# When the next batches' gate statistics are taken in a scan and expert kernel: split, moved behind the shared sums, with GpSimd's base additions held back

## The chip, the core and the metric

The kernel runs on one core of one Trainium2 chip. The metric is the device time of one execution in microseconds. Each kernel is run several times and the median counts; lower is better.

## What is computed

The input x is 4 batches of 512 tokens by 512 features. The first layer is a selective scan over the context, gated by SiLU of the normalized x; its result is added to x. The second layer normalizes again, runs two shared experts on all tokens and the two best of 16 routed experts on each token, and adds both:

```python
x = x + _L0_xattn_ref(ctx_1024, _layernorm(x, axis=-1), ...)   # scan output times silu(layernorm(x))
x = x + _L0_ffn_ref(_layernorm(x, axis=-1), ...)
# inside _L0_ffn_ref, with xn the normalized input:
aff = sigmoid(xn @ wa);  topk_p, topk_i = top_k(aff, 2)        # routing
routed = einsum('bsed,bse->bsd', experts(xn), combine)
shared = sum over 2 shared experts of w2(gelu(xn g + gb) * (xn w1 + b1)) + b2
return xn + shared + routed
```

## The kernel before, in words

The program has one instruction list for each engine, written out by hand, and semaphores between them: an instruction that waits holds up all that stands behind it on its engine. It has three stages. The first is projections and the scan (64 steps, to about 430 us). The second, the middle stage from about 430 to 640 us, goes through the four batches b = 0 to 3, each of four tiles of 128 tokens (16 tiles in all). The third runs 47 blocks of routed experts and adds their rows to the output.

The change lies in the middle stage. What each engine does there for batch b:

- **VectorE**, `first_norm(b)`: mean and variance of x for the gate (four BN_STATS of L930, four BN_AGGR of L933, then variance plus epsilon, L936), then a wait for GpSimd's reciprocal root (L454, `rstd_first(b)`), then the shift, minus mean times root (L938). ScalarE's `gates(b)` (L739, four SiLU activations with that scale and shift) waits for it.
- **TensorE**, `turn_gates(b)` (L1461): 16 transposes of the gates to PSUM; **VectorE**, `gate_tiles(b)` (L1017): four products of the scan's output with the transposed gates; `residual(b)` (L1025, L1027, L1029): adds x and takes the second norm's statistics; `variance(b)` (L1033); then GpSimd's `rstd_second(b)` (L496); then `normed(b)` (L1045), four tiles of the normalized tokens xn.
- **TensorE**, `turn_normed(b)` (L1489); ScalarE and VectorE split its result in two parts (`turn_normed` L749, `token_rests` L1053).
- The shared experts: TensorE's `up_shared(i)`, four of them for a batch (i = 0 to 15), 24 matmuls each; ScalarE's `gelu(i)` (L756) and `hidden_heads(i)` (L763); VectorE's `hidden_shared(i)` (L1066) and `hidden_rests(i)` (L1059). Then the down product, 12 matmuls (L1497, L1498, L1499) for a tile, into one of two PSUM banks by turns: `down_two_tiles(0, range(2))` for tiles 0 and 1, `down_shared(0, range(2, 4))` for tiles 2 and 3. VectorE's `add_shared` (L1075) adds each tile's sum out of its bank to `acc`; **TensorE starts a tile only when the tile two before it has been added**, since it needs that bank.
- **GpSimd**, `base(b)`: eight additions (L502 of xn, L504 of the shared bias, by turns) that make `acc` the base of the output. `add_shared` waits for those of its own batch.
- `logits(b)` on TensorE (12 matmuls with `wa_head`, `wa_rest`) needs all gates of batch b+1 applied; its 16 rows are copied by ScalarE (`copy_scores` L768), transposed by TensorE (L1516) and copied again (`copy_logits` L772).

The order on VectorE and GpSimd around the change is this (the rest is in the listing):

```python
            first_norm(2)
            first_norm(3)
            add_shared(0, every)
            gate_tiles(2)
...
            base(0)
            rstd_second(1)
            rstd_first(2)
            base(1)
            rstd_first(3)
            rstd_second(2)
            base(2)
```

Of the kernel before, what the change touches and what calls it, by code (L numbers as in the profile page):

```python
# [33 lines left out]
LT = L // P  # L34
# [16 lines left out]
def bass_xattn_scan_moe_kernel(nc, x, ctx_t, in_proj_t, conv_w, conv_b, x_proj_t, dt_proj_t, dt_b,  # L51
# [6 lines left out]
    with ExitStack() as ctx:  # L58
# [82 lines left out]
        def one_pass(ap):  # L141

            return ap.bitcast(F32R)
# [144 lines left out]
        def since(eng, semaphore, count):  # L288

            if not (isinstance(count, int) and count <= 0):  # L290
                eng.wait_ge(semaphore, count)
# [122 lines left out]
        def _(pool):  # L414
            s = S
# [34 lines left out]
            def rstd_first(b):  # L450

                pool.wait_ge(s["ln1_var"], b + 1)
                since(pool, s["gate_ready"], EC * b)
                pool.tensor_tensor(rstd[:], var_eps[:], minus_half[:], ALU.pow).then_inc(s["ln1_rstd"], 1)  # L454
# [39 lines left out]
            def rstd_second(b):  # L494
                pool.wait_ge(s["ln2_var"], b + 1)
                pool.tensor_tensor(rstd2[:], var_eps2[:], minus_half[:], ALU.pow).then_inc(s["ln2_rstd"], 1)  # L496

            def base(b):
                for i, lt in enumerate(TILES[b]):
                    t = b * LT + lt  # L500
                    pool.wait_ge(s["xn_ready"], b * LT + i + 1)
                    pool.tensor_tensor(acc[:, t], acc[:, t], xn[b % 2][:, lt], ALU.add).then_inc(s["base_xn"], 1)  # L502
                    pool.wait_ge(s["base_xn"], b * LT + i + 1)
                    pool.tensor_tensor(acc[:, t], acc[:, t], sb2_sb[:, 0], ALU.add).then_inc(s["base_ready"], 1)  # L504
# [10 lines left out]
            rstd_second(1)  # L515
            rstd_first(2)
            base(1)
            rstd_first(3)
            rstd_second(2)
            base(2)  # L520
            rstd_second(3)
            base(3)
# [54 lines left out]
        def _(act):  # L577
            s = S
# [154 lines left out]
            def gates(b):  # L733
                act.wait_ge(s["ln1_ready"], b + 1)
                if b == 0:
                    act.wait_ge(s["decay_ready"], EC * STEPS)
                since(act, s["gt_ready"], LT * b)
                for ec in range(EC):
                    act.activation(gates_of[b][:, ec], xb[b % 2][:, ec], ACT.Silu, bias=shift[:, ec:ec + 1],  # L739
                                   scale=rstd[:, ec:ec + 1]).then_inc(s["gate_ready"], 1)  # L740

            def turn_normed(b):
                for i, lt in enumerate(TILES[b]):
                    act.wait_ge(s["xnt_ready"], b * LT + i + 1)
                    if b >= 2:

                        act.wait_ge(s["sh_ready"], SH * FC * (b - 1))
                        act.wait_ge(s["scores_ready"], b - 1)
                    act.copy(one_pass(x_head[b % 2][:, :, lt * P:(lt + 1) * P]), ps[:, SIDE_BANK[lt]].rearrange(  # L749
                        "p (k n) -> p k n", n=P)).then_inc(s["xnt_copied"], 1)  # L750

            def gelu(i):
                q = i % (SH * FC)
                act.wait_ge(s["sh_ready"], i + 1)
                since(act, s["sy_ready"], i - 1)
                act.activation(sg[:, i % 2], ps[:, 2 * (i % 2)], ACT.Gelu,  # L756
                               bias=sbg_sb[:, q // FC, q % FC:q % FC + 1]).then_inc(s["sg_ready"], 1)

            def hidden_heads(i):
                q = i % (SH * FC)  # L760
                act.wait_ge(s["sy_ready"], i + 1)
                since(act, s["so_ready"], LT * (i // (SH * FC)))
                act.copy(one_pass(sy_head[:, q]), raw_hidden(i)).then_inc(s["syh_made"], 1)  # L763

            def copy_scores(b):
                act.wait_ge(s["scores_ready"], b + 1)
                since(act, s["logits_ready"], LT * (b - 1))
                act.copy(scores[b % 2], ps[0:E, SIDE_BANK[1]]).then_inc(s["scores_copied"], 1)  # L768
# [24 lines left out]
            gelu(4)  # L793
            gelu(5)
            hidden_heads(4)
            gates(3)
            copy_scores(1)
            copy_logits(1, 1)
            gelu(6)
            hidden_heads(5)  # L800
            turn_normed(2)
            gelu(7)
            hidden_heads(6)
            gelu(8)
# [79 lines left out]
        def _(dve):  # L884
            s = S
# [13 lines left out]
            def one_and_lost(b):  # L899
                e_b, one_b = e_abs[:, b % 2], one_e[:, b % 2]  # L900
                dve.wait_ge(s["exp_made"], b + 1)
                since(dve, s["delta_ready"], b - 1)
                dve.tensor_scalar(one_b, e_b, 1.0, None, ALU.add).then_inc(s["onep_made"], 1)
                dve.wait_ge(s["onep_made"], b + 1)
                dve.scalar_tensor_tensor(out=e_b, in0=one_b, scalar=-1.0, in1=e_b, op0=ALU.add,
                                         op1=ALU.subtract).then_inc(s["lost_made"], 1)

            def less_lost(b):
                dve.wait_ge(s["lost_made"], b + 1)
                dve.wait_ge(s["relu_made"], EC * (b + 1))  # L910
                dve.tensor_tensor(delta[:, b], delta[:, b], e_abs[:, b % 2], ALU.subtract).then_inc(s["relu_less"], 1)
# [11 lines left out]
                dve.wait_ge(s["dskip_made"], EC * (b + 1))  # L923
                dve.tensor_tensor(u[:, b], delta[:, b], u[:, b], ALU.mult).then_inc(s["du_made"], 1)

            def first_norm(b):

                dve.wait_ge(s["x_odd" if b % 2 else "x_even"], 16 * (b // 2 + 1))
                for ec in range(EC):
                    dve.bn_stats(stats[:, ec], xb[b % 2][:, ec]).then_inc(s["ln1_stat"], 1)  # L930
                dve.wait_ge(s["ln1_stat"], EC * (b + 1))
                for ec in range(EC):
                    dve.bn_aggr(meanvar[:, ec], stats[:, ec]).then_inc(s["ln1_aggr"], 1)  # L933
                dve.wait_ge(s["ln1_aggr"], EC * (b + 1))
                since(dve, s["gate_ready"], EC * b)
                dve.tensor_scalar(var_eps[:], meanvar[:, :, 1], EPS, None, ALU.add).then_inc(s["ln1_var"], 1)  # L936
                dve.wait_ge(s["ln1_rstd"], b + 1)
                dve.scalar_tensor_tensor(out=shift[:], in0=meanvar[:, :, 0], scalar=-1.0, in1=rstd[:],  # L938
                                         op0=ALU.mult, op1=ALU.mult).then_inc(s["ln1_ready"], 1)
# [6 lines left out]

            one_and_lost(0)
            less_lost(0)
            first_norm(0)
            one_and_lost(1)  # L950
            add_logarithm(0)
            delta_u(0)
# [82 lines left out]
            def normed(b):  # L1035
                dve.wait_ge(s["ln2_rstd"], b + 1)
                if b == 0:
                    dve.wait_ge(s["y_turned"], EC * STEPS)
                if b >= 2:

                    dve.wait_ge(s["xn_odd_stored" if b % 2 else "xn_even_stored"], 16 * LT * (b // 2))
                    dve.wait_ge(s["xnt_ready"], LT * (b - 1))
                    dve.wait_ge(s["base_xn"], LT * (b - 1))
                for lt in TILES[b]:
                    dve.tensor_scalar(xn[b % 2][:, lt], acc[:, b * LT + lt], meanvar2[:, lt, 0:1], rstd2[:, lt:lt + 1],  # L1045
                                      ALU.subtract, ALU.mult).then_inc(s["xn_ready"], 1)
# [14 lines left out]
            def hidden_shared(i):  # L1061
                q = i % (SH * FC)
                dve.wait_ge(s["sg_ready"], i + 1)
                if i not in AHEAD_OF_DOWN:
                    since(dve, s["so_ready"], LT * (i // (SH * FC)))
                dve.scalar_tensor_tensor(out=raw_hidden(i), in0=ps[:, 2 * (i % 2) + 1],  # L1066
                                         scalar=sb1_sb[:, q // FC, q % FC:q % FC + 1], in1=sg[:, i % 2],
                                         op0=ALU.add, op1=ALU.mult).then_inc(s["sy_ready"], 1)

            def add_shared(b, tiles):  # L1070
                for lt in tiles:
                    t = b * LT + lt
                    dve.wait_ge(s["so_ready"], t + 1)
                    dve.wait_ge(s["base_ready"], LT * (b + 1))
                    dve.tensor_tensor(acc[:, t], ps[:, 6 + lt % 2], acc[:, t], ALU.add).then_inc(s["so_added"], 1)  # L1075
# [126 lines left out]
            every, early, late = range(LT), range(LT // 2), range(LT // 2, LT)  # L1202
# [2 lines left out]
            variance(0)  # L1205
            normed(0)
            token_rests(0)
            first_norm(1)
            hidden_shared(0)
            gate_tiles(1)  # L1210
            residual(1, early)
# [8 lines left out]
            hidden_rests(2)  # L1220
            token_rests(1)
            hidden_rests(3)
            first_norm(2)
            first_norm(3)
            add_shared(0, every)
            gate_tiles(2)
            residual(2, early)
            hidden_shared(4)
# [2 lines left out]
            hidden_shared(5)  # L1231
            hidden_rests(4)
            normed(2)
            hidden_shared(6)
            hidden_rests(5)
            token_rests(2)
# [524 lines left out]
```

## Time and profile before

| what | value |
|---|---|
| median of 3 runs | 918.79 us (918.78 to 921.83) |
| profiled execution, its own time | 924.07 us |
| its span in the trace | 922.3 us |
| busy: TensorE / VectorE / ScalarE / GpSimd | 88% / 72% / 60% / 56% |

The profile is of one execution. Times in the trace count from the start of its span; 1.8 us of the execution's time lie outside it. PE is TensorE, PEld its weight loads, DVE VectorE, ACT ScalarE, POOL GpSimd, SP the queue that issues loads and stores. A matmul of 512 columns is shown with its modelled end, so that neighbours overlap: their pace is the distance of their starts.

### The profile page before, as it was taken

What the parts mean: (1) busy time and instruction counts of PE and PEld (TensorE: products, weight loads), DVE (VectorE), ACT (ScalarE), POOL (GpSimd) and SP (SyncE); (2) the same over time, 40 slices, a digit from 0 to 9 for tenths busy, and PEclk for the clock granted to TensorE, in tenths of its full rate; (3) what the DMA queues carried; (4) which work ended last, traced back from release to release, by engine and by line L of the source; (5) the groups of instructions that cost most, each with busy time, mean ns of one, the idle gap of its engine ahead of it and who ended that gap; (6) DMA issues with size and microseconds to landing.
All of it is one profiled execution on the core that took longest, in us unless ns stands there. A gap on an engine that the chain in (4) does not pass through costs nothing.

```text
span 922.3 us, 16039 instructions
## 1 busy us (share of the span) xinstructions
PE 815.4 (88%) x4380; PEld 594.0 (64%) x4381; DVE 663.1 (72%) x858; ACT 557.0 (60%) x927; POOL 520.0 (56%) x326
## 2 busy tenths in 40 slices
PE   6987489999999988996885999999999899989992
PEld 2323378888888878886764778886555455545550
DVE  4859889999999998999584585825555565545551
ACT  3588499999999999994331422113554455545541
POOL 2310079999999999997813542022254535356432
PEclk9976699999999999999897999999999999999997
DMA  5010031111141113201220112059367787777773
GB/s 169 0 51 1 1 125 56 55 56 54 59 139 56 58 47 104 59 12 56 83 92 0 46 47 92 6 177 411 81 172 221 181 212 173 203 177 211 181 166 50
DMA packets 32424, 95.44 MB, mean 103 GB/s; under 512 B 5088, under 2 KB 5216, under 8 KB 29040
## 3 DMA queue, kind: packets, MB, share of 16 engines
q1 hardware_dynamic: 20400, 65.37, 21.1%
q0 software_dynamic: 11968, 29.37, 14.7%
q8 instruction: 30, 0.49, 0.2%
q14 instruction: 26, 0.21, 0.1%
HBM read 122.11 MB, written 21.36 MB: 156 GB/s over the span
## 4 chain that ended last, share of the span: by engine, by line
PE 45%; DVE 17%; DMA 16%; POOL 9%; issue 8%; ACT 3%; POOLq 1%; DVEq 0%; SPq 0%; ACTq 0%
DVE r L979 12%; DMA out<-sg,ids 7%; DMA out<-sb_sb,ids 6%; PE ps L1497 6%; PE ps L1499 6%; PE ps L1498 6%; POOL r L464 5%; PE ps L1422 5%; PE ps L1446 5%; PE ps L1671 3%; PE ps L1353 3%; PE ps L1423 3%; PE ps L1652 3%; PE ps L1361 2%; DMA r<-xn_scratch,ids 2%
## 5 line engine op out<-in xcount | busy, mean ns | idle before, releaser
L464 POOL TENSOR_TENSOR r<-r,mem 128x1024 f32<-128x1024 f32 x126 | 295.2, 2384 | 55.5 <-DMA mem<-cm_rows 51.8
L979 DVE TENSOR_TENSOR_SCAN r<-r,ps 128x1024 f32<-128x1024 f32 x128 | 286.9, 2277 | 15.8 <-issue 10.2
L684 ACT ACTIVATE r<-mem,nega 128x511 f32<-128x511 f32 x256 | 167.1, 711 | 1.1 <-DVE r L979 1.1
L1422 PE MATMUL ps<-ident,mem 128*128 128x128 f32 x768 | 131.5, 281 | 30.3 <-DVE r L979 22.4
L1446 PE MATMUL ps<-ident,r 128*128 128x128 f32 x1024 | 132.6, 273 | 1.2 <-POOL r L464 1.0
L696 ACT ACTIVATE mem<-mem,bc 128x512 f32<-128x512 f32 x192 | 124.6, 712 | 10.0 <-PE ps L1423 9.4
L1422 PEld LDWEIGHTS ps<-ident,mem 128*128 128x128 f32 x768 | 88.3, 143 | 55.6 <-issue 53.3
L1446 PEld LDWEIGHTS ps<-ident,r 128*128 128x128 f32 x1024 | 115.8, 141 | 2.0 <-POOL r L464 1.5
L1423 PE MATMUL ps<-mem 128*128 128x128 f32 x512 | 100.7, 279 | 0.0
L1671 PE MATMUL ps<-mem 128*128 x188 | 92.3, 616 | 2.0 <-ACT mem L846 1.4
L1497 PE MATMUL ps<-split 128*128 128x512 f32 x192 | 78.8, 411 | 16.3 <-DVE acc L1075 12.2
L1652 PE MATMUL ps<-r,picked 128*128 x188 | 88.3, 592 | 0.0
L1423 PEld LDWEIGHTS ps<-mem 128*128 128x128 f32 x512 | 79.0, 195 | 0.0
L569 POOL DMA_INDIRECT out<-sg,ids x24 | 38.9, 1620 | 68.9 <-DMA out<-sg,ids 28.0
L1499 PE MATMUL ps<-split 128*128 128x512 f32 x192 | 76.9, 400 | 0.0
L1498 PE MATMUL ps<-split 128*128 128x512 f32 x192 | 76.7, 399 | 0.0
L569 POOL DMA_INDIRECT out<-sb_sb,ids x23 | 37.5, 1629 | 66.2 <-DMA out<-sb_sb,ids 30.7
L1278 DVE TENSOR_TENSOR acc_again<-r,acc_again 128x1024 fp32r<-128x1024 f32 x47 | 57.6, 1226 | 20.5 <-issue 20.2
L537 POOL DMA_INDIRECT r<-xn_scratch,ids x47 | 53.3, 1134 | 31.9 <-PE ps L1638 19.0
L837 ACT CAST acc_again<-r 128x1024 fp32r x47 | 49.0, 1046 | 33.2 <-issue 21.1
L756 ACT ACTIVATE sg<-ps,sbg_sb 128x512 f32<-128x512 f32 x16 | 10.9, 689 | 92.8 <-PE ps L1499 92.8
L846 ACT COPY mem<-ps 128x256 f32<-128x256 f32 x47 | 17.5, 372 | 68.9 <-PE ps L1660 68.7
(195 smaller groups left out, 1323.0 us busy)
## 6 DMA issues: line engine op xcount, KB each, us to landing
r<-in_r_up SPq DMA_DIRECT2D x47, 1024.0 KB
mem<-in_r_down SPq DMA_DIRECT2D x47, 512.0 KB
mem<-cm_rows SPq DMA_DIRECT2D x64, 256.0 KB, 3.3
mem<-in_r_b SPq DMA_DIRECT2D x4, 2048.0 KB, 14.0
r<-in_x SPq DMA_DIRECT2D x4, 1024.0 KB, 4.8
xn_scratch<-r SPq DMA_DIRECT2D x16, 256.0 KB, 2.8
out<-acc POOLq DMA_DIRECT2D x16, 256.0 KB, 2.9
mem<-in_ctx_t SPq DMA_DIRECT2D x4, 512.0 KB, 8.3
```

The costliest lines, as they stand in the source:

```text
L464: pool.tensor_tensor(state[:, k % 2, ec:ec + 2], state[:, k % 2, ec:ec + 2], c, ALU.mult).then_inc(s["weighed"], 1)
L684: act.activation(decay[:, k % 2, ec, 1:L], delta[:, b, ec, 1:L], ACT.Exp, scale=nega[:, ec, n:n + 1]).then_inc(s["decay_ready"], 1)
L696: act.activation(dbu_t[:, k % 2, lt], du_t[:, t], ACT.Copy, scale=bc[:, t, DR + k % DS:DR + k % DS + 1]).then_inc(s["dbut_made_a"], 1)
L979: dve.tensor_tensor_scan(state[:, half, ec:ec + 2].rearrange("p e l -> p (e l)"), decay[:, half, ec:ec + 2].rearrange("p e l -> p (e l)"), ...
L1422: pe.transpose(ps[:, ec, lt * P:(lt + 1) * P], dbu_t[:, k % 2, lt, ec * P:(ec + 1) * P], ident[:])
L1423: pe.matmul(ps[:, ec, (LT - 1) * P:LT * P], du_t[:, k // DS * LT + LT - 1, ec * P:(ec + 1) * P], b_diag[k % 2], start=True, stop=True).the ...
L1446: mm = pe.matmul(ps[:, Y_BANK + lt, ec * P:(ec + 1) * P], state[:, k % 2, ec, lt * P:(lt + 1) * P], ident[:], is_transpose=True, start=Fal ...
L1497: pe.matmul(to, one_pass(l_head), one_pass(r_head), start=(first and i == 0), stop=False)
L1498: pe.matmul(to, one_pass(l_head), one_pass(r_rest), start=False, stop=False)
L1499: mm = pe.matmul(to, one_pass(l_rest), one_pass(r_head), start=False, stop=(last and i == n - 1))
L1652: mm = pe.matmul(ps[:, r % 2], xgt[:, r % 2, (kc - KSPLIT) * P:(kc - KSPLIT + 1) * P], up_weights(slot_j, kc, kc + 1), start=False, stop=( ...
L1671: mm = pe.matmul(ps[:, 6 + r % 2], hyt[:, r % 2, fc * P:(fc + 1) * P], down_weights(slot_j, fc), start=(fc == 0), stop=(fc == FC - 1))
```

## The change

VectorE's `first_norm(b)` becomes two functions: `first_stats(b)`, which ends with the variance, and `first_shift(b)`, which waits for GpSimd's root and makes the shift. For batches 0 and 1 they are called one right after the other, as before. For batch 2 the sums of tiles 0 and 1 are added between them and those of tiles 2 and 3 behind. For batch 3 both are moved behind `normed(2)`. On ScalarE `gates(3)` moves from behind `hidden_heads(4)` to behind `turn_normed(2)`. On GpSimd `rstd_second(2)` and `rstd_first(3)` change places, and each `base(b)` waits once, for all four tiles of xn of its batch, where it waited tile by tile.

```diff
             def base(b):
+                pool.wait_ge(s["xn_ready"], LT * (b + 1))
                 for i, lt in enumerate(TILES[b]):
                     t = b * LT + lt
-                    pool.wait_ge(s["xn_ready"], b * LT + i + 1)
                     pool.tensor_tensor(acc[:, t], acc[:, t], xn[b % 2][:, lt], ALU.add).then_inc(s["base_xn"], 1)
...
             base(1)
+            rstd_second(2)
             rstd_first(3)
-            rstd_second(2)
             base(2)
...
             hidden_heads(4)
-            gates(3)
             copy_scores(1)
             copy_logits(1, 1)
             gelu(6)
             hidden_heads(5)
             turn_normed(2)
+            gates(3)
             gelu(7)
...
-            def first_norm(b):
+            def first_stats(b):
...
                 dve.tensor_scalar(var_eps[:], meanvar[:, :, 1], EPS, None, ALU.add).then_inc(s["ln1_var"], 1)
+
+            def first_shift(b):
+
                 dve.wait_ge(s["ln1_rstd"], b + 1)
...
             hidden_rests(3)
-            first_norm(2)
-            first_norm(3)
-            add_shared(0, every)
+            first_stats(2)
+            add_shared(0, early)
+            first_shift(2)
+            add_shared(0, late)
             gate_tiles(2)
...
             normed(2)
+            first_stats(3)
+            first_shift(3)
             hidden_shared(6)
```

VectorE where the sums of batch 0 are added, before: `x4` is four instructions of a kind; BN_STATS of `r` is the statistics of x, `acc<-ps,acc` of L1075 the sums, of L1017 the gate products.

```order
L936 TENSOR_SCALAR var_eps<-meanvar 128x4
L938 SCALAR_TENSOR_TENSOR shift<-meanvar,rstd 128x4
L930 BN_STATS stats<-r 128x6 x4
L933 BN_AGGR meanvar<-stats 128x2 x4
L936 TENSOR_SCALAR var_eps<-meanvar 128x4
L938 SCALAR_TENSOR_TENSOR shift<-meanvar,rstd 128x4
L1075 TENSOR_TENSOR acc<-ps,acc 128x512 x4
L1017 TENSOR_TENSOR acc<-ps,acc 128x512 x4
```

The same place in the changed kernel, whose lines from here on have numbers four higher (three for the shift):

```order
L936 TENSOR_SCALAR var_eps<-meanvar 128x4
L1079 TENSOR_TENSOR acc<-ps,acc 128x512 x2
L941 SCALAR_TENSOR_TENSOR shift<-meanvar,rstd 128x4
L1079 TENSOR_TENSOR acc<-ps,acc 128x512 x2
L1021 TENSOR_TENSOR acc<-ps,acc 128x512 x4
```

Two sums now stand ahead of batch 2's shift, and nothing of batch 3 stands ahead of any sum.

VectorE after `variance(2)` in the changed kernel, where batch 3's part has gone; L1049 is `normed(2)`, L1070 `hidden_shared`, L1063 `hidden_rests`:

```order
L1070 SCALAR_TENSOR_TENSOR mem<-ps,sb_sb,sg 128x512
L1063 TENSOR_TENSOR split<-mem,split 128x512
L1049 TENSOR_SCALAR r<-acc,meanvar,rstd 128x512 x4
L930 BN_STATS stats<-r 128x6 x4
L933 BN_AGGR meanvar<-stats 128x2 x4
L936 TENSOR_SCALAR var_eps<-meanvar 128x4
L941 SCALAR_TENSOR_TENSOR shift<-meanvar,rstd 128x4
L1070 SCALAR_TENSOR_TENSOR mem<-ps,sb_sb,sg 128x512
```

Before, the last row followed right on `normed(2)`.

ScalarE, the difference from `hidden_heads(4)` on; ACT_TABLE_LOAD changes between the tables of SiLU and GELU, the four ACTIVATE of L739 are `gates(3)`:

```order
 L763 CAST split<-mem 128x512
+L768 COPY picked<-ps 16x512
+L772 COPY aff<-ps 128x64
+L756 ACTIVATE sg<-ps,sbg_sb 128x512
+L763 CAST split<-mem 128x512
+L749 CAST split<-ps 128x4x128 x4
 L739 ACT_TABLE_LOAD
 L739 ACTIVATE r<-r,shift,rstd 128x512 x4
-L768 COPY picked<-ps 16x512
-L772 COPY aff<-ps 128x64
 L756 ACT_TABLE_LOAD
-L756 ACTIVATE sg<-ps,sbg_sb 128x512
```

The gates of batch 3 and both table loads now stand between `turn_normed(2)` (L749) and `gelu(7)`; their number is the same.

GpSimd, the difference behind `base(1)`:

```order
 L502 TENSOR_TENSOR acc<-acc,r 128x512
 L504 TENSOR_TENSOR acc<-acc,sb_sb 128x512
-L454 TENSOR_TENSOR rstd<-var_eps,minus_half 128x4
-L496 TENSOR_TENSOR rstd<-var_eps,minus_half 128x4
+L496 TENSOR_TENSOR rstd<-var_eps,minus_half 128x4
+L454 TENSOR_TENSOR rstd<-var_eps,minus_half 128x4
 L502 TENSOR_TENSOR acc<-acc,r 128x512
```

The root for the second norm of batch 2 now comes ahead of the root for the gate of batch 3, and both still ahead of `base(2)`.

## Rows read from the trace of the kernel before

**Rows 1.** Whom TensorE waited for, 460 to 645 us: total, times, longest.

```profile
PE ps L1497 <- DVE acc L1075: 12.2, 1, 12.2
...
PE ps L1516 <- ACT picked L768: 0.5, 1, 0.5
```

**Rows 2.** Stretches: length, busy PE, PEld, DVE, ACT, POOL, clock, DMA share, GB/s.

```profile
481.80:494.00 12.20, 0.01 (x2) 0.01 (x1) 5.65 (x13) 4.21 (x5) 11.02 (x10) 0.62 0.00 0
494.00:498.40 4.40, 4.40 (x10) 3.46 (x11) 0.54 (x1) 0.00 (x0) 0.00 (x0) 0.51 0.00 0
498.40:560.00 61.60, 60.28 (x301) 46.26 (x300) 38.95 (x64) 18.97 (x31) 27.12 (x24) 1.00 0.15 56
560.00:656.00 96.00, 95.50 (x452) 75.31 (x451) 55.10 (x148) 23.36 (x45) 14.26 (x19) 0.98 0.41 159
656.00:922.30 266.30, 241.28 (x845) 138.51 (x843) 139.10 (x214) 127.73 (x255) 120.92 (x85) 0.97 0.70 173
```

**Rows 3.** Timeline of VectorE, 480 to 505 us: start, length, what, [idle before].

```profile
480.64 0.17 DVE L936 TENSOR_SCALAR var_eps<-meanvar 128x4 f32<-128x4 f32 x1
481.94 1.21 DVE L938 SCALAR_TENSOR_TENSOR shift<-meanvar,rstd 128x4 f32<-128x4 f32 x1 [1.12 <-POOL rstd L454]
...
486.22 0.85 DVE L936 TENSOR_SCALAR var_eps<-meanvar 128x4 f32<-128x4 f32 x1 [0.27 <-ACT r L739]
493.17 0.16 DVE L938 SCALAR_TENSOR_TENSOR shift<-meanvar,rstd 128x4 f32<-128x4 f32 x1 [6.11 <-POOL rstd L454]
493.25 1.29 DVE L1075 TENSOR_TENSOR acc<-ps,acc 128x512 f32<-128x512 f32 x2
```

**Rows 4.** Timeline of GpSimd: end of `base(0)`, start of `base(1)`, batch 3's root.

```profile
457.12 1.28 POOL L504 TENSOR_TENSOR acc<-acc,sb_sb 128x512 f32<-128x512 f32 x1
...
481.87 1.26 POOL L502 TENSOR_TENSOR acc<-acc,r 128x512 f32<-128x512 f32 x1
...
492.12 1.02 POOL L454 TENSOR_TENSOR rstd<-var_eps,minus_half 128x4 f32<-128x4 f32 x1
```

**Rows 5.** Timeline of TensorE at its waits.

```profile
476.12 0.47 PE L1497 MATMUL ps<-split 128*128 128x512 f32 x1 [1.66 <-issue]
...
480.74 0.39 PE L1499 MATMUL ps<-split 128*128 128x512 f32 x1
...
481.42 0.39 PE L1499 MATMUL ps<-split 128*128 128x512 f32 x1
494.00 0.79 PE L1497 MATMUL ps<-split 128*128 128x512 f32 x1 [12.19 <-DVE acc L1075]
...
530.88 1.91 PE L1461 MATMUL ps<-ident,r 128*128 128x128 f32 x16
```

**Rows 6.** Timeline of ScalarE, 515 to 532 us.

```profile
515.68 1.28 ACT L739 ACT_TABLE_LOAD   x1
516.97 2.94 ACT L739 ACTIVATE r<-r,shift,rstd 128x512 f32<-128x512 f32 x4
...
524.97 2.05 ACT L749 CAST split<-ps 128x512 fp32r<-128x512 f32 x4
531.09 0.69 ACT L756 ACTIVATE sg<-ps,sbg_sb 128x512 f32<-128x512 f32 x1 [4.06 <-PE ps L1499]
```

**Rows 7.** Timeline of VectorE: gate products, normalizations, and a `hidden_shared`.

```profile
457.50 2.47 DVE L1017 TENSOR_TENSOR acc<-ps,acc 128x512 f32<-128x512 f32 x4
...
469.67 1.91 DVE L1045 TENSOR_SCALAR r<-acc,meanvar,rstd 128x512 f32<-128x512 f32 x4 [0.48 <-POOL rstd L496]
...
516.45 3.87 DVE L1045 TENSOR_SCALAR r<-acc,meanvar,rstd 128x512 f32<-128x512 f32 x4
524.60 0.75 DVE L1066 SCALAR_TENSOR_TENSOR mem<-ps,sb_sb,sg 128x512 f32<-128x512 f32 x1 [4.28 <-ACT sg L756]
...
533.07 2.48 DVE L1017 TENSOR_TENSOR acc<-ps,acc 128x512 f32<-128x512 f32 x4
...
543.00 3.87 DVE L1045 TENSOR_SCALAR r<-acc,meanvar,rstd 128x512 f32<-128x512 f32 x4
```

More of the change, by code:

```diff
@@ L948, in _ @@
             less_lost(0)
-            first_norm(0)
+            first_stats(0)
+            first_shift(0)
             one_and_lost(1)
@@ L1207, in _ @@
             token_rests(0)
-            first_norm(1)
+            first_stats(1)
+            first_shift(1)
             hidden_shared(0)
```

## The prediction, made before the changed kernel was run

> **What bounds the kernel now.** I read TensorE's waits first. In the middle stage it has one large wait: 12.2 us for VectorE's sum of L1075, and nothing else near it [rows 1]. The table of stretches shows the same from outside: between 481.8 and 494.0 us TensorE does nothing while VectorE is busy for 5.65 us and GpSimd for 11.02 [rows 2]. In the 4.4 us behind it the granted clock is 0.51, TensorE's lower level of 1.2 GHz; from 498.4 to 560 it is 1.00, the upper level of 2.4 GHz, and TensorE is busy 60.28 of 61.60 us, then 95.50 of 96.00 to 656 us [rows 2]. So behind this one hole TensorE sets the pace until the experts run, and a microsecond taken out of the hole should move everything behind it, as long as the others keep up.
>
> VectorE's timeline tells what fills the hole. The reader should follow the order: batch 2's variance ends at 480.81, its shift comes at 481.94; batch 3's variance comes at 486.22; then VectorE stands still for 6.11 us until 493.17, waiting for GpSimd's root L454; only then come the sums, at 493.25 [rows 3]. GpSimd's timeline tells why the root is late: `base(1)` starts at 481.87 and the root of batch 3 is queued behind its eight additions, at 492.12 [rows 4]. TensorE had ended tiles 0 and 1 at 481.42 + 0.39 = 481.81, and started tile 2 at 494.00, right behind tile 0's sum [rows 5].
>
> **The hole, step by step.** Now the sums of tiles 0 and 1 stand right behind batch 2's variance, so VectorE is free for them from 480.81 [rows 3]. Tile 0's last matmul starts at 480.74 and ends at 481.13 [rows 5]. A sum takes about 0.69 us with its start-up (two take 1.29) [rows 3], so tile 0 is added at about 481.85 and tile 1 at 482.5. TensorE, done at 481.81, goes on at about 481.9. Gain: 494.0 - 481.9 = 12.1 us.
>
> **The clock.** Behind the hole ten matmuls take 4.4 us at the lower clock [rows 2]; at the pace before the hole, (481.42 - 480.74) / 3 = 0.227 us, they take 2.3 [rows 5]. That is 2.1 us more to gain if the clock stays up. A short pause does not take it down here: the one of 1.66 us before 476.12 is followed by matmuls of 0.39 us at 0.227 us distance [rows 5]. With 0.1 us instead of 12.2 I count the 2.1 us as gained.
>
> **Batch 2's gates.** The root of batch 2 is unchanged (the shift still waits for it, and base(1) starts at 481.87 as before [rows 4]). The shift took 1.21 us at 481.94, beside an addition of GpSimd that ran from 481.87 to 483.13, against 0.16 for the same shift at 493.17 with a root beside it [rows 3, 4]. Standing behind tile 1's sum it would end at about 483.2, as it did before: 0. ScalarE's gates then end near 486.1 (2.94 us, [rows 6]), and TensorE wants them after tiles 2 and 3, at 481.9 + 24 x 0.227 = 487.3. Hidden with 1.2 us to spare. Tile 3 is added at about 488.2, in time for `turn_gates(2)`'s last tile. The gate products follow, 2.5 us [rows 7]; the first residual addition behind them, near 490.8, can meet the last addition of `base(1)`, which ends at 492.1 [rows 4], and lose up to 1.3 us. Behind it stands `hidden_shared(4)`, which has to wait for the 24 matmuls of `up_shared(4)` in any case, to about 494.8, and whose reader is two up products away: 0.
>
> **GpSimd behind it.** `base(1)` still ends at 492.1. The root of batch 2's second norm is asked for ahead of `normed(2)` at 516.45 [rows 7], after the change some 14 us earlier, at 500 to 502. GpSimd has been idle for 7 us by then: 0.
>
> **Batch 3's part in its new place.** From here on times are those of before, since all is moved by the same amount. `normed(2)` takes 3.87 us with GpSimd's additions beside it, `normed(1)` 1.91 without [rows 7]. As `base(2)` now waits for all four tiles, it should take 1.9, to 518.4. Statistics and variance cost about 3.1 us (from 483.15, the end of one shift, to 486.22 [rows 3]), to 521.4; the root comes 1.3 us later (480.64 to 481.94 [rows 3]) and the shift may be held by the first addition of `base(2)`, so to 522.9 or 523.9. VectorE was idle for 4.28 us until 524.60 there [rows 7]: it fits, with 0.7 us left. What is queued behind the new wait is `hidden_shared(6)`, whose reader, TensorE's up product two further on, is 5 us away.
>
> **Batch 3's gates.** ScalarE ends `turn_normed(2)` at 524.97 + 2.05 = 527.02 [rows 6]. A table load, 1.28 us, and four gates, 2.94 [rows 6], end at 531.24. TensorE begins `turn_gates(3)` at 530.88 [rows 5], with weights loaded just ahead: it waits 0.4 to 0.6 us. Against that, `copy_scores(1)` no longer stands behind `gates(3)`, so the wait of 0.5 us of L1516 goes [rows 1], and it moves ScalarE earlier too. The two cancel: 0, give or take 0.3. The second load pushes `gelu(7)` from 531.09 [rows 6] to 532.5, 1.4 us late, and with it VectorE's gate products from 533.07 to 534.5, ending at 537.0 instead of 535.55 [rows 7]. TensorE needs them for `logits(2)`, which it reaches after 16 transposes and 24 matmuls, 530.88 + 1.9 + 5.4 = 538.2 (estimate from [rows 5]): 1.2 us to spare. `normed(3)` starts up to 1.5 us after 543.00 but takes 1.9 instead of 3.87 us [rows 7], so it ends at 546.4, before the 546.87 of now. `base(3)` starts 3 us later relative to the rest; the stores and loads behind it wait for later things.
>
> The row has the SiLU load at 515.68 with 1.28 us and the first gate at 516.97, right on its end [rows 6]. The Trainium skill, "ScalarE: Activation LUTs", section "What ACT_TABLE_LOAD costs", puts a switch at about 2.66 us, since a drain of 1.38 us follows the load. By that page, as an estimate, `gates(3)` would end 1.4 us later and the gain be 12.8 instead of 14.2; the trace here does not agree.
>
> **Sum.** 12.1 + 2.1 + 0 = 14.2 us. The profiled execution's own time is 924.07, so 909.9 for it. That execution was 5.3 us above the median; the hole is a matter of order, not of that surplus, so I take the same 14.2 from the median: 918.79 - 14.2 = **904.6 us**, 1.5% faster. About 0.5% (4.6 us) is what a measurement of this kernel can tell from no change.
>
> **Rivals.**
> - **Held gates.** The load and gates in their new place cost more than their rows say, for instance 1.4 us more before the first gate; TensorE then waits about 2 us at `turn_gates(3)`. For: it is the tightest new meeting, with no slack at all. Against: the row at 516.97. Gain 12.8, 906.0 us. Chance 0.05.
> - **The clock falls elsewhere.** A lower clock for about 4 us comes back at another place, for instance at the 0.5 us waits or in the routing. For: 560 to 656 has a mean of 0.98, so there is one such place already [rows 2]. Gain 12.1, 906.7 us. Chance 0.07.
> - **The sums still come late.** VectorE's sums or batch 2's shift run slower beside `base(1)`, so that TensorE loses 3 to 5 us of the 14. Against: the gate products have the operands of the sums, and beside `base(0)`'s additions at 457.50 [rows 4] they took 2.47 us, without any at 533.07 the same 2.48 [rows 7]. 908 to 910 us. Chance 0.05.
> - **The expert stage takes it back.** From 656 us on TensorE is busy 241.28 of 266.30 us and the DMA share is 0.70 [rows 2]; if that stage kept its end whatever its start, up to all 14 us would go. Against: all its loads are released by events of the middle stage. 911 to 919 us. Chance 0.05, half of it within 0.5%.
> - **No hole closed.** Another wait of the same kind, for instance of TensorE for the gates of batch 2, takes its place at once: 918 us. It needs these gates 12 us later than ScalarE can give them; nothing in rows 3 and 6 says so. Chance 0.02.
> - **Slower.** The mechanism is batch 3's shift behind `normed(2)`. ScalarE reaches its gates at 528.3, the shift is there by 523.9. Each microsecond beyond 528.3 holds TensorE at `turn_gates(3)`; only a shift later than about 542.5 eats the 14.2 us, and 20 us later than reckoned gives 920 us and more. The root would have to stand behind `base(2)`, and it stands ahead. Chance 0.02.
> - **More than forecast**, 16 us and over, by fewer small waits: 0.02, about 902 us.
>
> The forecast has the rest, 0.72; its own range is 902 to 908, since the three runs shown lie up to 3 us apart.
>
> **The numbers.** The range 901 to 908.5 takes in the forecast, the held gates, the other clock and the larger gain, 0.86 less what the runs' own spread puts outside. Faster by over 0.5%, below 914.2: 0.72 + 0.05 + 0.07 + 0.05 + 0.02 and half of 0.05 = 0.935. Within 0.5%: 0.045. Slower: 0.02.
>
> **What the new profile would show.** TensorE's wait for L1079 (the old L1075) at about 481.8 below 0.5 us, and matmuls at 0.227 us distance with a granted clock of 1.00 through 482 to 498. VectorE's first two sums at about 481.2, its shift right behind. The 16 transposes of `turn_gates(2)` starting near 487.5. `normed(2)` and `normed(3)` at 1.9 us. `gates(3)` ending about when TensorE asks for it. The end of the middle stage 14 us earlier, and a last stage of unchanged length. I would be wrong if TensorE showed a new wait of over 1 us at L1461 or at the logits, if VectorE's sums took twice their time beside GpSimd, or if the last stage grew.

## The result, and the profile after

The changed kernel takes 904.24 us (median of 4 runs, 898.68 to 907.32) against 918.78 (median of 4, 915.33 to 921.83) beside it. The ratio is 0.9846, with a 95% interval of 0.9816 to 0.9876: 1.5% faster, 14.5 us by the medians, where 14.2 were forecast. Its profiled execution took 904.82 us, its span is 903.0.

TensorE's waits in the changed kernel, 440 to 645 us (total, times, longest); the first is the one at the start of the middle stage, which was there before and which I had not looked at:

```profile
PE ps L1497 <- DVE r L1049: 7.5, 1, 7.5
...
PE ps L1469 <- ACT r L739: 0.3, 1, 0.3
```

The wait of 12.2 us for the sum, and that of 0.5 for ScalarE's copy [rows 1], are gone; a new one of 0.3 us for the gates of batch 3 (L1469) has come. The stretches of [rows 2], in the new trace (busy PE, PEld, DVE, ACT, POOL, then clock, DMA share, GB/s):

```profile
481.80:494.00 12.20, 12.10 (x61) 9.91 (x61) 7.88 (x14) 4.22 (x5) 11.52 (x9) 1.00 0.00 0
484.00:546.00 62.00, 60.88 (x303) 46.57 (x303) 39.89 (x75) 22.34 (x36) 35.86 (x31) 1.00 0.11 40
546.00:642.00 96.00, 95.58 (x457) 74.95 (x455) 55.78 (x149) 24.89 (x46) 15.37 (x23) 1.00 0.44 170
```

Where TensorE was busy for 0.01 us of 12.2, it is busy for 12.10, at a granted clock of 1.00. VectorE at the same place, to be held against [rows 3] (this trace runs 1.1 us later up to here):

```profile
481.73 0.17 DVE L936 TENSOR_SCALAR var_eps<-meanvar 128x4 f32<-128x4 f32 x1
482.29 1.37 DVE L1079 TENSOR_TENSOR acc<-ps,acc 128x512 f32<-128x512 f32 x2 [0.39 <-PE ps L1507]
483.58 0.69 DVE L941 SCALAR_TENSOR_TENSOR shift<-meanvar,rstd 128x4 f32<-128x4 f32 x1
486.09 0.69 DVE L1079 TENSOR_TENSOR acc<-ps,acc 128x512 f32<-128x512 f32 x1 [1.82 <-PE ps L1507]
488.82 0.69 DVE L1079 TENSOR_TENSOR acc<-ps,acc 128x512 f32<-128x512 f32 x1 [2.04 <-PE ps L1507]
```

VectorE now waits for TensorE (0.39, 1.82, 2.04 us) and not the other way round. TensorE in the same stretch and at its two later meetings, against [rows 5]:

```profile
477.21 0.47 PE L1505 MATMUL ps<-split 128*128 128x512 f32 x1 [1.66 <-issue]
...
482.54 0.39 PE L1507 MATMUL ps<-split 128*128 128x512 f32 x1
483.04 0.50 PE L1505 MATMUL ps<-split 128*128 128x512 f32 x1
...
488.62 1.91 PE L1469 MATMUL ps<-ident,r 128*128 128x128 f32 x16
...
517.79 1.97 PE L1469 MATMUL ps<-ident,r 128*128 128x128 f32 x16 [0.29 <-ACT r L739]
...
536.63 0.50 PE L1505 MATMUL ps<-split 128*128 128x512 f32 x1 [0.83 <-DVE split L1057]
```

Tiles 0 and 1 end at 482.54 + 0.39 = 482.93, tile 2 starts at 483.04: 0.1 us.

**Two marks.** To compare all traces I cut each in three. H is the time up to the first matmul of the down product of batch 0, the one behind the wait of 1.66 us (476.12 before, 477.21 after). M runs from the end of tiles 0 and 1, 5.7 us later, to the first matmul behind the wait of 0.83 us for batch 3's token rests (549.69 before, 536.63 after). L is the rest of the span. From before to after, H grows by 1.1 us, M falls from 67.9 to 53.7, by 14.2, and L falls from 372.6 to 366.4, by 6.2: together the 19.3 us between the two spans. The medians differ by 14.5, so one of these numbers had to be scatter. The table has the traces of all runs.

| kernel | H | M | L | time, median (runs) |
|---|---|---|---|---|
| before | 476.1 | 67.9 | 372.6 | 918.78 (4) |
| changed | 477.2 | 53.7 | 366.4 | 904.24 (4) |
| e0, changed again | 478.6 | 53.7 | 363.2 | 900.91 (4) |
| e1, before, root first | 476.2 | 61.7 | 366.9 | 911.97 (10) |
| e2, changed, gates(3) in the old place | 477.5 | 63.2 | 365.2 | 912.41 (10) |
| e3, changed, batch 2 not split | 476.3 | 57.2 | 364.4 | 904.57 (4) |
| e4, changed, additions tile by tile | 478.2 | 53.7 | 364.7 | 903.18 (4) |
| e5, before, hole filled | 478.4 | 66.1 | 364.4 | 915.74 (10) |
| e6, changed, warm start | 475.7 | 53.7 | 364.6 | 901.54 (6) |
| e7, changed again | 476.0 | 53.7 | 364.6 | 905.97 (6) |
| e8, e6 again | 476.0 | 53.7 | 362.1 | 903.47 (6) |
| e9, e3 with the second wait filled | 477.3 | 55.6 | 363.8 | 904.20 (1) |
| e10, e3 with the first wait filled | 477.8 | 57.2 | 363.9 | 906.40 (1) |

M repeats to 0.1 us for one kernel (53.7 in three traces of the changed one). In the same three traces H moves by 2.6 us and L by 3.2. The reader should judge a change of this stage by M: the three medians of the changed kernel (904.24, 900.91 and 905.97) lie 5 us apart.

### The profile page after: what moved, and what is told of

Read it like the earlier page. It is cut to its first block, busy times and chain, and to the rows that moved or that the text cites. A ratio compares the mean times of both kernels' runs of the same rounds, so it can differ in the third digit from the quotient of the medians.

```text
span 903.0 us, 16039 instructions
## 1 busy us (share of the span) xinstructions
PE 809.5 (90%) x4380; PEld 589.3 (65%) x4381; DVE 659.1 (73%) x858; ACT 556.4 (62%) x927; POOL 521.0 (58%) x326
## 4 chain that ended last, share of the span: by engine, by line
PE 43%; DMA 17%; DVE 15%; issue 9%; POOL 9%; ACT 5%; POOLq 1%; DVEq 0%; SPq 0%; ACTq 0%
DVE r L983 11%; DMA out<-sg,ids 8%; DMA out<-sb_sb,ids 8%; PE ps L1505 6%; PE ps L1506 6%; PE ps L1507 6%; POOL r L464 5%; PE ps L1430 5%; PE ps L1454 5%; PE ps L1361 3%; PE ps L1431 3%; PE ps L1369 2%; PE ps L1679 2%; PE ps L1660 2%; ACT mem L696 2%
## 5 line engine op out<-in xcount | busy, mean ns | idle before, releaser
L464 POOL TENSOR_TENSOR r<-r,mem 128x1024 f32<-128x1024 f32 x126 | 295.2, 2380 | 57.2 <-DMA mem<-cm_rows 53.9
L1505 PE MATMUL ps<-split 128*128 128x512 f32 x192 | 77.4, 403 | 4.2 <-DVE split L1057 2.3
L1506 PE MATMUL ps<-split 128*128 128x512 f32 x192 | 75.6, 394 | 0.0
L1507 PE MATMUL ps<-split 128*128 128x512 f32 x192 | 75.4, 393 | 0.0
```

The lines of the kernel that those rows point to most:

```text
L464: pool.tensor_tensor(state[:, k % 2, ec:ec + 2], state[:, k % 2, ec:ec + 2], c, ALU.mult).then_inc(s["weighed"], 1)
L1505: pe.matmul(to, one_pass(l_head), one_pass(r_head), start=(first and i == 0), stop=False)
L1506: pe.matmul(to, one_pass(l_head), one_pass(r_rest), start=False, stop=False)
L1507: mm = pe.matmul(to, one_pass(l_rest), one_pass(r_head), start=False, stop=(last and i == n - 1))
```

## The experiments

The theory: VectorE's sums stood behind batch 3's shift, this behind a root queued on GpSimd behind eight additions; taking that away gives 12.1 us, and 2.1 more by the clock. The rivals: the gain comes from fewer collisions of VectorE and GpSimd, from the move on ScalarE, or from the expert stage.

**e0, the changed kernel again.**

> The changed kernel once more, as the yardstick. Two marks are read in each trace. M: from the modelled end of the last matmul of tiles 0 and 1 of batch 0 (481.81 us before, 482.93 after) to the first matmul behind the wait for batch 3's token rests (549.69 before, 536.63 after): 67.9 us before, 53.7 after. L: from that matmul to the span's end, 372.6 us before, 366.4 after. My theory: the change is worth the 14.2 us of M, and the 6.2 us of L are scatter from run to run of the expert stage, so L here lies anywhere from 365 to 374. Rival: the change shortens L too; then L is 366 to 367 here and in every kernel that keeps the new order.

M is 53.7 again, L is 363.2, below the 366 to 367 of the rival. Two kernels with the old order, e1 and e5, have an L of 366.9 and 364.4. So nothing shows that the change touches L. The times say the same: over all runs the mean is 918.1 for the kernel before (51 runs) and 903.3 for the changed one (14), 14.9 us apart, give or take 2.

The 372.6 of the first profile was a long execution (924.07 us, 5.3 over its median). A part of its surplus can be read from the clock. Between 550 and 870 us the clock falls to its lower level for some 3 us three times in that trace, twice in e1, once in those of the changed kernel and e4, and not at all in the other nine, e5 with the old order among them. The first fall in the kernel before (stretch as in [rows 2]):

```profile
574.00:576.00 2.00, 2.00 (x6) 1.52 (x6) 1.83 (x7) 0.00 (x0) 0.00 (x0) 0.50 0.00 0
```

TensorE had no wait around it: the trace shows none from 560 to 600 us. The ten matmuls from 573.04 us on take 3.97 us, where they take 2.3 at the usual distance, so one such fall costs some 1.6 us. Why it comes in some executions and not in others stays open, as does the rest of the surplus.

**e1, GpSimd's additions of batch 1 behind batch 3's root, in the kernel before.**

```diff
-            base(1)
             rstd_first(3)
+            base(1)
             rstd_second(2)
```

> The kernel before, with one line moved on GpSimd: base(1) stands behind batch 3's root instead of ahead of it. VectorE and ScalarE keep the old order. Theory (the root queued behind eight additions makes most of the hole): batch 2's shift no longer meets an addition (0.2 instead of 1.2 us), batch 3's variance comes at about 485.2, its root ends at 486.4, the first sum starts at 486.6, TensorE goes on at 487.3. Hole 5.5 us instead of 12.2, M about 61.2 with the lower clock behind the hole, 59.1 without; time 912 to 914. Rival (the hole is VectorE's own work, or the gain came from fewer collisions of VectorE with GpSimd): hole over 10 us, M over 66.

The hole is 6.5 us instead of 12.2, M 61.7, the time 911.97 us (ratio 0.9943, 0.9914 to 0.9971). VectorE and TensorE in this kernel:

```profile
485.25 0.17 DVE L936 TENSOR_SCALAR var_eps<-meanvar 128x4 f32<-128x4 f32 x1 [0.27 <-ACT r L739]
486.54 1.21 DVE L938 SCALAR_TENSOR_TENSOR shift<-meanvar,rstd 128x4 f32<-128x4 f32 x1 [1.12 <-POOL rstd L454]
487.67 1.27 DVE L1075 TENSOR_TENSOR acc<-ps,acc 128x512 f32<-128x512 f32 x2
```

```profile
488.40 0.80 PE L1497 MATMUL ps<-split 128*128 128x512 f32 x1 [6.52 <-DVE acc L1075]
```

One line on GpSimd takes half the hole away: the queue is the cause of that half. My 5.5 us were 1.0 short because I let batch 3's shift run freely; it met the first addition of `base(1)`, now right behind its root, and took 1.21 us. M fell by 6.2 us, 0.5 more than the hole, as the slow stretch behind it ends after 3.3 us (near 491.7) and not after 4.4. What is left of the hole is VectorE's own order: batch 3's statistics and shift still stand ahead of the sums, and e3 below shows what goes with them.

**e2, the changed kernel with gates(3) in its old place on ScalarE.**

```diff
             hidden_heads(4)
+            gates(3)
             copy_scores(1)
...
             turn_normed(2)
-            gates(3)
             gelu(7)
```

> The changed kernel with gates(3) back in its old place on ScalarE, behind hidden_heads(4). Theory: ScalarE stands at gates(3) until batch 3's shift (about 510.8), copies the scores at about 513.7, and TensorE, which wants them at 506.9, waits 7.4 us there and runs 4 us at the lower clock: M 53.7 + 7.4 + 2.1 = 63.2, time 912 to 915. Rival (the move on ScalarE is of no account): M within 0.5 of 53.7.

M is 63.2, as worked out, and the time 912.41 us. TensorE's wait and the slow matmul behind it:

```profile
514.43 0.61 PE L1524 MATMUL ps<-ident,picked 16*128 16x16 f32 x4 [7.23 <-ACT picked L768]
514.97 0.80 PE L1505 MATMUL ps<-split 128*128 128x512 f32 x1
515.56 0.63 PE L1506 MATMUL ps<-split 128*128 128x512 f32 x1
```

So without the move on ScalarE the change would give back 9.5 of its 14.2 us: what waits for a step that is moved has to move with it. What that move would bring by itself no run shows. The swap of the two roots on GpSimd has no run of its own either, and could not have one: with batch 3's variance behind `normed(2)`, a `rstd_first(3)` ahead of `rstd_second(2)` would wait for that variance, `normed(2)` stands ahead of it, and `normed(2)` waits for `rstd_second(2)`: the three would wait for each other.

**e3, the changed kernel without batch 2's split.**

```diff
             first_stats(2)
-            add_shared(0, early)
             first_shift(2)
+            add_shared(0, early)
             add_shared(0, late)
```

> The changed kernel with batch 2's shift ahead of all sums again (its statistics not in two parts; batch 3's stay behind normed(2)). Theory: the shift waits for its root to 483.0 and for GpSimd's first addition to 484.2, the first sum ends at 484.95, TensorE waits 2.0 us instead of 0.1 and keeps its clock: M 55.7, time 2 us over the changed kernel, too little to tell by medians of three. So 12.1 of the 14.2 us are batch 3's doing. Rival (splitting batch 2 is the main part): M over 60.

TensorE waits for 1.97 us, as expected, yet M is 57.2 and not 55.7. TensorE, then two stretches of this kernel (columns as in [rows 2]):

```profile
481.65 0.39 PE L1507 MATMUL ps<-split 128*128 128x512 f32 x1
484.01 0.50 PE L1505 MATMUL ps<-split 128*128 128x512 f32 x1 [1.97 <-DVE acc L1079]
484.35 0.40 PE L1506 MATMUL ps<-split 128*128 128x512 f32 x1
484.59 0.40 PE L1507 MATMUL ps<-split 128*128 128x512 f32 x1
484.82 0.52 PE L1505 MATMUL ps<-split 128*128 128x512 f32 x1
485.13 0.63 PE L1506 MATMUL ps<-split 128*128 128x512 f32 x1
```

```profile
484.00:486.00 2.00, 1.99 (x7) 1.56 (x8) 0.55 (x1) 2.00 (x4) 1.94 (x2) 0.74 0.00 0
486.00:488.50 2.50, 2.50 (x8) 2.00 (x7) 0.00 (x0) 1.60 (x2) 2.48 (x2) 0.53 0.00 0
```

After the pause three matmuls run at full pace; then the distance becomes 0.43 us until 488.1. The clock fell one microsecond after TensorE had resumed. So the split is worth 3.5 us (2.0 of waiting and 1.5 of clock), and 10.7 of the 14.2 come from taking batch 3's part away from the sums, with all that has to move with it. The median, 904.57, could not have told this.

**e9 and e10, which pause took the clock down.** The pause of 1.97 us comes 7.7 us behind another, of 1.66 us. e9 fills the later one, e10 the earlier, with matmuls that nobody reads:

```diff
             down_two_tiles(0, range(2))
+            for _ in range(8):
+                pe.matmul(ps[:, 0], one_pass(sup_head[:, 0, 0, 0:P]), one_pass(x_head[0][:, 0]), start=True, stop=True)
             down_shared(0, range(2, LT))
```

```diff
+            pe.wait_ge(s["sy_ready"], 3)
+            for _ in range(6):
+                pe.matmul(ps[:, 0], one_pass(sup_head[:, 0, 0, 0:P]), one_pass(x_head[0][:, 0]), start=True, stop=True)
             down_two_tiles(0, range(2))
```

> The kernel without batch 2's split (sums behind the shift), with 8 unread matmuls in TensorE's 2.0 us wait for the first sum. Theory (that wait, coming 7.7 us behind another of 1.7 us, takes the clock down): all matmuls behind it at 0.227 us distance, M 55.7 instead of 57.2. Rival (the drop has another cause): slow matmuls remain behind it, M 57.2.

> The same kernel without the split, the 2.0 us wait left as it is, and 6 unread matmuls in the 1.7 us wait ahead of the down product. If the 2.0 us pause alone takes the clock down, the slow matmuls stay and M is 57.2. If it takes both pauses, the clock stays up and M is 55.7.

e9 has M 55.6 and no slow matmul. e10 has M 57.2, and the slow ones stay. e9, then e10:

```profile
482.84 1.97 PE L1610 MATMUL ps<-split 128*128 128x512 f32 x8
485.01 0.50 PE L1505 MATMUL ps<-split 128*128 128x512 f32 x1 [0.19 <-DVE acc L1079]
485.35 0.39 PE L1506 MATMUL ps<-split 128*128 128x512 f32 x1
```

```profile
485.45 0.50 PE L1505 MATMUL ps<-split 128*128 128x512 f32 x1 [1.97 <-DVE acc L1079]
...
486.48 0.52 PE L1506 MATMUL ps<-split 128*128 128x512 f32 x1
486.79 0.63 PE L1507 MATMUL ps<-split 128*128 128x512 f32 x1
```

Filled, the pause of 1.97 us is not followed by a fall; filling the one of 1.66 us changes nothing. So the fall hangs on the later pause, as far as one trace of each kernel can tell. It is not a matter of the length alone: e6 and e8, below, have a pause of 1.98 us with no fall behind it. What else decides stays open.

**e4, the changed kernel with GpSimd's additions tile by tile.**

```diff
             def base(b):
-                pool.wait_ge(s["xn_ready"], LT * (b + 1))
                 for i, lt in enumerate(TILES[b]):
                     t = b * LT + lt
+                    pool.wait_ge(s["xn_ready"], b * LT + i + 1)
```

> The changed kernel with base(b) waiting tile by tile again, as before. Theory (the wait for all four tiles only moves additions out of the way of VectorE, and that time is hidden): normed(2) and normed(3) take 3.9 us each again instead of 1.9, batch 3's shift slips by 2 us into VectorE's idle time, M 53.7 to 54.4. Rival (fewer collisions are a good part of the gain): M 57 or more.

M is 53.7, as in the changed kernel. The one wait for four tiles, the part of the change that its title names last, is worth nothing measurable here. But my expectation missed half of what happens. VectorE's two normalizations in e4, and GpSimd between them:

```profile
504.55 1.91 DVE L1049 TENSOR_SCALAR r<-acc,meanvar,rstd 128x512 f32<-128x512 f32 x4
...
509.53 1.01 POOL L454 TENSOR_TENSOR rstd<-var_eps,minus_half 128x4 f32<-128x4 f32 x1 [6.57 <-DVE var_eps L936]
...
532.40 3.86 DVE L1049 TENSOR_SCALAR r<-acc,meanvar,rstd 128x512 f32<-128x512 f32 x4 [0.91 <-POOL rstd L496]
```

Only `normed(3)` takes 3.86 us again (1.92 in the changed kernel). `normed(2)` stays at 1.91: `base(2)` stands behind batch 3's root, and that root now waits for a variance behind `normed(2)`. It is the reordering that keeps `base(2)` away from `normed(2)`; the single wait only matters for `normed(3)`, whose 2 us are hidden.

**e5, the kernel before with its hole filled.** All waits stay; between tiles 1 and 2 TensorE runs 50 matmuls that nobody reads.

```diff
             down_two_tiles(0, range(2))
+            for _ in range(50):
+                pe.matmul(ps[:, 0], one_pass(sup_head[:, 0, 0, 0:P]), one_pass(x_head[0][:, 0]), start=True, stop=True)
             down_shared(0, range(2, LT))
```

> The kernel before, with 50 matmuls of 512 columns, whose result nobody reads, put into TensorE's hole behind tiles 0 and 1 (11.4 of 12.2 us). All waits stay. Theory (behind the hole 2.1 us are lost to the lower clock): granted clock 1.00 from 482 to 500, the next sum's matmuls at 0.227 us distance, M 67.9 - 2.1 = 65.8. Rival (the slow matmuls behind the hole have another cause, such as VectorE's or GpSimd's traffic): they stay at 0.43 us and M at 67.9.

Stretches of this kernel, the hole and what follows:

```profile
484.10:496.40 12.30, 11.26 (x50) 9.01 (x48) 5.71 (x13) 4.22 (x5) 11.18 (x10) 1.00 0.00 0
496.40:501.00 4.60, 4.55 (x20) 3.76 (x21) 1.29 (x2) 0.00 (x0) 0.00 (x0) 1.00 0.00 0
```

The clock stays at 1.00, against 0.51 behind the empty hole [rows 2], and M falls by 1.8 us, to 66.1. The matmuls are useless and the kernel is faster for them: 915.74 us against 917.21 (ratio 0.9970, 0.9951 to 0.9989). Of the 14.2 us some 2 are the clock's.

**e6 and e8, a warm start on top of the changed kernel.** The waits of the changed kernel point to the 7.5 us ahead of batch 0's transposes. The hole itself is the chain of the first normalization; what can be had is the slow clock behind it.

```diff
             pe.wait_ge(s["loaded_shared"], 16 * 4)
+            pe.wait_ge(s["wh_made"], len(SPLIT_AT))
+            pe.wait_ge(s["gated"], LT)
+            for _ in range(25):
+                pe.matmul(ps[:, 0], one_pass(sup_head_all[:, 0:P]), one_pass(sup_head_all[:, 0:L]), start=True, stop=True)
             turn_normed(0)
...
-            for c in range(2, 6):
+            for c in range(2, 4):
                 weight_rests(c)
             rstd_first(1)
+            for c in range(4, 6):
+                weight_rests(c)
```

> The changed kernel, and on top of it 25 matmuls of 512 columns, whose result nobody reads, in TensorE's 7.5 us wait for the first normalized tile (432.3 to 439.8), and GpSimd's root for batch 1's gate taken behind two of the four subtractions of weights instead of behind all four. Theory: the transposes of batch 0 (3.65 us at the lower clock) take 1.9, the wait for batch 0's token rests ends 1.7 us sooner, the first eight matmuls save 1.6 us: the middle stage starts 3.3 us sooner, M and L unchanged, time 3 us under the changed kernel. Rival: batch 1's gates or GpSimd's subtractions hold TensorE a little later, and less than 1 us is left.

> The changed kernel, side by side with the next run. M 53.7 and a time of 901 to 905. L is expected between 363 and 367 as in all traces but that of the kernel before, 372.6.

> The changed kernel with the 25 unread matmuls ahead of batch 0's transposes and GpSimd's root taken earlier, once more, side by side with the changed kernel. The trace of its first run has the middle stage 2.7 us shorter. Theory: its median lies 2 to 3.5 us under that of the changed kernel beside it. Rival (the saving is given back in the expert stage, or is only scatter): within 1 us of it.

e7 (changed), then e8:

```profile
438.79 3.65 PE L1497 MATMUL ps<-ident,r 128*128 128x128 f32 x16 [7.51 <-DVE r L1049]
443.93 0.77 PE L1505 MATMUL ps<-split 128*128 128x512 f32 x1 [1.49 <-DVE split L1057]
```

```profile
435.32 5.91 PE L1604 MATMUL ps<-split 128*128 128x512 f32 x25 [1.39 <-DVE acc L1023]
441.51 1.94 PE L1499 MATMUL ps<-ident,r 128*128 128x128 f32 x16 [0.28 <-DVE r L1051]
445.43 0.47 PE L1507 MATMUL ps<-split 128*128 128x512 f32 x1 [1.98 <-DVE split L1059]
```

The 16 transposes take 1.94 us instead of 3.65. From the first transpose of batch 0's gates to the first matmul of the down product it is 46.3 us in e6 (429.37 to 475.66) and e8 (429.73 to 476.04), and 48.9 in e0 (429.67 to 478.58): 2.6 us saved where I had 3.3, mostly since the wait for the token rests grew from 1.49 to 1.98. M and L do not answer. Side by side the medians are 903.47 and 905.97, 2.5 us apart; but the six runs of each lie from 899.34 to 909.45 and from 900.86 to 907.32, and over all runs the mean is 902.4 for the warm start (12 runs) and 903.3 for the changed kernel (14), 0.8 us apart, give or take 2.5. The traces show 2.6 us; the times agree with that and with nothing at all, so the 2.5 us between the two medians are no proof.

TensorE pauses for 1.98 us ahead of 445.43, and behind this pause the clock stays up (e8; e6 shows the same):

```profile
445.40:450.40 5.00, 4.97 (x22) 4.13 (x23) 3.81 (x10) 0.00 (x0) 4.17 (x3) 1.00 0.02 8
```

## Why the prediction was right

**The hole: right to 0.1 us.** I had TensorE wait 0.1 us behind tiles 0 and 1, and it waits 0.1. M fell by 14.2, the sum that I had. That the median, 904.24, came out 0.4 us from the forecast is luck: medians of this one kernel lie 5 us apart.

**The clock: right in the sum, thin in its reason.** The clock stayed up, and e5 shows about 2 us for it (1.8 against my 2.1). But I leaned on one pause of 1.66 us as proof that short pauses are harmless. In e3 and e10 the clock falls behind one of 1.97 us, in e6 and e8 not behind one of 1.98, and in the kernel before, near 574 us, it falls with no pause at all. So the length of a pause alone does not tell, and my reason was none. The gain held because the wait fell to 0.1 us; in e3, with VectorE 1.9 us later, 3.5 us went, not 2.

**Batch 2's gates: right.** The shift ended at 484.27, the 483.2 that I gave plus the 1.1 us by which this trace is later; it was held by an addition, 0.69 us instead of 0.16. TensorE began `turn_gates(2)` at 488.62 without a wait. ScalarE had ended the gates at 487.24, 1.4 us ahead, close to the 1.2 that I worked out; the 12 us of slack that I gave them under "No hole closed" contradict that and were wrong.

**Batch 3's part in its new place: right in the times, wrong in one reason.** `normed(2)` takes 1.91 us instead of 3.87 [rows 7], but not for the single wait in `base(2)` that I gave as the reason: e4, without it, has 1.91 too. The root ahead of `base(2)` holds it back. Further, the statistics end at 508.4, and the shift, held by the first addition of `base(2)` as I allowed, ends at 510.74. VectorE, from `normed(2)` on:

```profile
503.48 1.91 DVE L1049 TENSOR_SCALAR r<-acc,meanvar,rstd 128x512 f32<-128x512 f32 x4
505.30 2.46 DVE L930 BATCH_NORM_STATS2 stats<-r 128x6 f32<-128x512 f32 x4
...
508.21 0.17 DVE L936 TENSOR_SCALAR var_eps<-meanvar 128x4 f32<-128x4 f32 x1
509.50 1.24 DVE L941 SCALAR_TENSOR_TENSOR shift<-meanvar,rstd 128x4 f32<-128x4 f32 x1 [1.12 <-POOL rstd L454]
511.06 0.75 DVE L1070 SCALAR_TENSOR_TENSOR mem<-ps,sb_sb,sg 128x512 f32<-128x512 f32 x1 [0.32 <-ACT sg L756]
```

The margin was 0.32 us; I had 0.7.

**Batch 3's gates: right.** TensorE waits 0.29 us at L1469 and no longer at the copy of the scores (0.49 us before): the two cancel. ScalarE around it:

```profile
511.43 2.05 ACT L749 CAST split<-ps 128x512 fp32r<-128x512 f32 x4
513.50 1.28 ACT L739 ACT_TABLE_LOAD   x1
514.80 2.94 ACT L739 ACTIVATE r<-r,shift,rstd 128x512 f32<-128x512 f32 x4
517.75 1.28 ACT L756 ACT_TABLE_LOAD   x1
519.05 0.69 ACT L756 ACTIVATE sg<-ps,sbg_sb 128x512 f32<-128x512 f32 x1
```

Both loads are followed by an activation 0.02 us after their end. Each load begins right on the end of the instruction ahead of it, too (511.43 + 2.05 and 514.80 + 2.94). By the figures that I weighed from the Trainium skill, "ScalarE: Activation LUTs", section "What ACT_TABLE_LOAD costs", each load would be joined by a drain of 1.38 us, and TensorE would have waited for it; the trace does not agree.

**What I had not counted.** The title's last part, the single wait for four tiles, adds nothing (e4); I had taken its 2 us on VectorE as what made batch 3's part fit. The 2 us came from the reordering itself, so the fit with `normed(2)` at 3.87 us was never put to the test, and the margin of 0.32 us says nothing of more room. And I set the surplus of the profiled execution aside rightly: it was L, and 6 of the 19 us between the two profiles would have misled anyone who took the spans as the result.

## What to carry to other kernels

When an engine stands still for 12 us, follow the wait through two queues: the short step that is waited for may be queued behind long ones that nobody needs yet, and on the waiting engine the work that is due may stand behind a step that is not. Move the step that is not due, and with it whatever waits for it on other engines (e2: 9.5 us given back otherwise). Cut the trace at marks that all kernels share: here one stage repeats to 0.1 us, while whole runs scatter by several.

## What the runs showed of the hardware that I had not expected

- Behind a pause of TensorE of 1.97 us the clock fell from the upper level to the lower one (2.4 to 1.2 GHz) in e3 and e10, some 1 us after TensorE had resumed; it stayed down for 3 to 4 us, which cost 1.5 us. Behind a pause of 1.98 us it did not fall (e6, e8), nor behind those of 1.66 us in any trace. And it fell near 574 us in the kernel before with TensorE busy throughout, and likewise in e1 and e4.
- Useless matmuls in a wait that exists anyway can pay: 1.8 us at the hole (e5, where the times show a gain too), and 2.6 us at the start of the middle stage in the traces of e6 and e8, which the times do not tell from nothing.
- A VectorE instruction on 4 elements per partition takes 1.21 to 1.24 us instead of 0.16 when an addition of GpSimd has just begun (e1 and the changed kernel), and four of 512 elements 3.87 instead of 1.91 [rows 7]. Four products that read PSUM take 2.47 us with the additions beside them (at 457.50, while GpSimd adds until 461.0) and 2.48 without [rows 7].
